# A two-layer decoder on one core: cross queries as three 16-bit products, low values on GpSimd, the expert sum on two engines, a second set of self weights, and a new written order

## What is computed

```
x = x + self_attention0(layernorm(x))        16 heads of 8, causal
x = x + cross_attention0(layernorm(x), ctx)   8 heads of 64, with output bias
x = x + ternary_ffn(layernorm(x))             x rounded to 8 bit, weight rounded to -1, 0, 1
x = x + self_attention1(layernorm(x))        16 heads of 8, scores clipped to +-10, causal
x = x + cross_attention1(layernorm(x), ctx)  16 heads of 64
x = x + experts(layernorm(x))                 8 experts, softmax gate, those under 0.1 dropped
```

## Time and profile before

| | |
|---|---|
| median of 3 runs | 501.73 us (499.9 to 504.64) |
| profiled execution | 504.29 us, span 502.5 us, mean granted TensorE clock 0.983 |
| TensorE busy | 471.4 us, 94% |
| ScalarE busy | 438.6 us, 87% |
| VectorE busy | 404.4 us, 80% |
| GpSimd busy | 383.4 us, 76% |

### The profile page before, as it was taken

The page is one execution under the profiler, slowest core; times in us unless marked ns, Lnnn a source line. Parts: engine busy times, 40 slices in busy tenths (PEclk is TensorE's granted clock), DMA queues, the critical chain, the costliest instruction groups (busy, mean ns, idle before and its releaser), DMA issues.

```text
span 502.5 us, 16468 instructions
## 1 busy us (share of the span) xinstructions
PE 471.4 (94%) x5702; PEld 399.1 (79%) x5702; DVE 404.4 (80%) x954; ACT 438.6 (87%) x1180; POOL 383.4 (76%) x465
## 2 busy tenths in 40 slices
PE   7789998999999999999999999999999899999866
PEld 3678786787888898877888888897788788978764
DVE  4598887986888888888889898888987678867645
ACT  4688889999999989998989999999889898999842
POOL 2487587877668878889979888996877599775752
PEclk8799999998999999999999999999999999999989
DMA  6800222205132422531254215243424224233450
GB/s 195 330 3 3 43 43 44 43 10 115 24 68 45 85 44 42 94 65 39 48 92 87 55 29 79 44 90 46 85 53 84 57 44 86 43 65 71 89 97 16
DMA packets 107841, 33.87 MB, mean 67 GB/s; under 512 B 102768, under 2 KB 106224, under 8 KB 107760
## 3 DMA queue, kind: packets, MB, share of 16 engines
q1 hardware_dynamic: 107328, 32.04, 31.8%
q10 hardware_dynamic: 432, 0.79, 0.5%
HBM read 6.50 MB, written 1.05 MB: 15 GB/s over the span
## 4 chain that ended last, share of the span: by engine, by line
PE 59%; ACT 10%; POOL 9%; issue 9%; DMA 3%; POOLq 3%; DVE 3%; SPq 2%; DVEq 1%; ACTq 0%
PE psum L1291 6%; PE psum L1333 5%; PE psum L1419 5%; PE psum L1342 4%; POOL w_self L774 4%; PE psum L1322 4%; POOL e_parts_cross L781 3%; PE psum L1382 3%; ACT w_cross L865 3%; DMA eT_cross<-e_parts_cross 2%; PE psum L1431 2%; PE psum L1392 2%; PE psum L1373 2%; PE psum L1400 2%; PE psum L1355 2%
## 5 line engine op out<-in xcount | busy, mean ns | idle before, releaser
L774 POOL TENSOR_TENSOR w_self<-w_self 128x1024 f16<-128x1024 f32 x64 | 120.9, 1900 | 19.8 <-ACT w_self L854 14.3
L781 POOL TENSOR_TENSOR e_parts_cross<-w_cross,e_parts_cross 128x1024 f16<-128x1024 f32 x48 | 102.6, 2141 | 13.0 <-ACT e_parts_cross L874 13.0
L865 ACT ACTIVATE w_cross<-psum,row_max_cross 128x128 f32<-128x128 f32 x384 | 105.0, 413 | 3.7 <-DVE row_max_cross L1045 3.4
L1045 DVE TENSOR_REDUCE row_max_cross<-psum 128x8 f32<-128x1024 f32 x48 | 58.3, 1219 | 7.9 <-PE psum L1333 7.5
L1333 PE MATMUL psum<-kT_cross,qT_cross 64*128 64x128 f32 x768 | 54.7, 284 | 0.6 <-ACT qT_cross L830 0.6
L1333 PEld LDWEIGHTS psum<-kT_cross,qT_cross 64*128 64x128 f32 x768 | 46.4, 187 | 8.4 <-issue 5.2
L874 ACT ACTIVATE e_parts_cross<-w_cross 128x1024 f16<-128x1024 f32 x48 | 52.6, 1099 | 0.3
L1373 PE MATMUL psum<-v_high_cross,eT_cross 128*128 128x65 bf16 x384 | 40.6, 196 | 5.5 <-DMA eT_cross<-e_parts_cross 3.7
L1373 PEld LDWEIGHTS psum<-v_high_cross,eT_cross 128*128 128x128 f16 x384 | 35.7, 98 | 10.5 <-issue 8.9
L1083 DVE SCALAR_TENSOR_TENSOR w_self<-psum,s_bound 128x1024 f32<-128x1024 f32 x32 | 37.9, 1219 | 4.3 <-PE psum L1322 3.6
L1072 DVE TENSOR_REDUCE row_max_self<-psum 128x8 f32<-128x1024 f32 x32 | 38.9, 1216 | 2.9 <-PE psum L1322 2.8
(11 more groups left out here) (221 smaller groups left out, 1539.9 us busy)
## 6 DMA issues: line engine op xcount, KB each, us to landing
eT_cross<-e_parts_cross SPq DMA_TRANSPOSE x96, 3.1
out_dram<-x_all SPq DMA_DIRECT2D x16, 64.0 KB, 2.0
x_all<-in_x SPq DMA_DIRECT2D x1, 768.0 KB, 7.8
cT_all<-in_ctx SPq DMA_DIRECT2D x1, 768.0 KB, 9.6
e_k<-in_e_k SPq DMA_DIRECT2D x1, 512.0 KB, 5.5
e_v<-in_e_v SPq DMA_DIRECT2D x1, 512.0 KB, 6.4
e_q<-in_e_q SPq DMA_DIRECT2D x1, 512.0 KB, 8.6
e_o<-in_e_o SPq DMA_DIRECT2D x1, 512.0 KB, 9.6
```

The source lines that it names most:

```text
L774: pool.tensor_tensor(L.w_low[u], L.w[u][:], halves(L.w[u][:]), ALU.subtract)\
L781: pool.tensor_tensor(L.e_parts[u][:, UN:2 * UN], L.e[u][:], L.e_parts[u][:, 0:UN], ALU.subtract)\
L865: last = act.activation(L.e[u][:, P * p:P * (p + 1)], S_[:, P * p:P * (p + 1)], ACT.Exp, bias=L.row_max[:, u, p:p + 1])
L1045: dve.tensor_reduce(L.row_max[:, u, :], group(i, turn)[:].rearrange("p (h k) -> p h k", h=UNIT), AX_X, ALU.max, negate=True).then_inc(L.ma ...
```

## The change

Five edits, with new costs in `all_steps` and a new `ORDER` for every engine:

1. Queries: the weight is scaled by 4096 and split once into a bf16 high part (ScalarE, `b_q.hi` and `e_q.hi`) and an fp16 low part (VectorE, `b_q.lo` and `e_q.lo`); `xnT` of the cross stages is fp16, with an fp16 remainder `xnT_low` made by a new VectorE step `xl`. A query step has twelve 16-bit products instead of four fp32 ones. ScalarE's copy out (`qe`) undoes the scale.
2. Values: ScalarE now writes them as fp32; the bf16 high and fp16 low parts are the upper and lower 16 bits of each 4-byte place, so `pv` reads both with a step of 4 bytes. cross1's `vl` moves to GpSimd; cross0's stays on VectorE.
3. Cross weights: `lo` writes its remainder over the first half of `w`, so the next `ex` waits until the transposing DMA of the remainder has landed (`e_turned`) and no longer for `e_low`; `lo` loses its own wait for that DMA.
4. First self attention: `w` exists twice (four tiles); `mx` waits for the `pv` of two sequences before, and `ex` loses its wait for the previous `pv`.
5. Experts: `ml` multiplies four experts in one instruction of 128x512 and adds the other four with four multiply-add instructions of 128x128; `sm` loses its first addition of 128x512.

`LOADS` puts `e_k`, `e_v` and `ctx` ahead of `more`. Some small tiles move into room that the new tiles leave. The new order keeps the shape of the old one: the same steps run on TensorE, ScalarE's order has the two `hi` steps more, VectorE's has `xl` and the two `lo` steps more and cross1's `vl` less, and GpSimd's has these.

```
+VECTOR_LOW = ("cross0",)
+Q_UNIT = 4096.0
...
-                add(f"{L}.mx.{u}", "DVE", 2430, [f"{L}.s1"], [f"{L}.t.{u}"])
+                add(f"{L}.mx.{u}", "DVE", 2430, [f"{L}.s1"], [ago(f"{L}.pv", 2)])
...
-    add("tern.make", "DVE", 2900, ["tern.sum"], once=True)
+    add("tern.make", "DVE", 5000, ["tern.sum"], once=True)
...
-                     more=["a_o", "b_q", "b_o", "b_bias", "f_w"], e_k=["e_k"], e_v=["e_v"], x=[], ctx=[],
+                     e_k=["e_k"], e_v=["e_v"], ctx=[], more=["a_o", "b_q", "b_o", "b_bias", "f_w"], x=[],
...
-        self.v_high = [self.sb(f"v_high{b}", [P, heads, XD + 1], BF16) for b in range(AHEAD[name])]
-        self.v_low = [self.sb(f"v_low{b}", [P, heads, XD], FP16) for b in range(AHEAD[name])]
+        self.v = [self.sb(f"v{b}", [P, heads, XD + 1]) for b in range(AHEAD[name])]
+        self.v_high = [by_halves(v, BF16)[:, :, :, 1] for v in self.v]
+        self.v_low = [by_halves(v, FP16)[:, :, 0:XD, 0] for v in self.v]
...
+        self.high_plane = [self.sb(f"high_plane{u}", [P, UN], FP16) for u in range(self.units)]
+        self.low_plane = [w[:].bitcast(FP16)[:, 0:UN] for w in self.w]
...
             def low_weights(L, i, u):
                 pool.wait_ge(L.e_high[u], i + 1)
-                if i:
-                    pool.wait_ge(L.e_turned[u], 16 * i)
-                pool.tensor_tensor(L.e_parts[u][:, UN:2 * UN], L.e[u][:], L.e_parts[u][:, 0:UN], ALU.subtract)\
+                pool.tensor_tensor(L.low_plane[u], L.e[u][:], L.high_plane[u][:], ALU.subtract)\
                     .then_inc(L.e_low[u], 1)
+            def low_values(L, i, u):
+                buffer, heads = i % AHEAD[L.name], slice(UNIT * u, UNIT * (u + 1))
+                pool.wait_ge(*emptied(i, f"{L.name}.v.{u}"))
+                pool.tensor_tensor(L.v_low[buffer][:, heads, :], L.v[buffer][:, heads, 0:XD],
+                                   L.v_high[buffer][:, heads, 0:XD], ALU.subtract).then_inc(L.v_split[u], 1)
...
-                pool.tensor_tensor(weighted[:, 0:4, :], weighted[:, 0:4, :], weighted[:, 4:8, :], ALU.add)
-                pool.drain()
...
                 act.wait_ge(L.max_ready[u], i + 1)
                 if i:
-                    act.wait_ge(L.e_low[u], i)
+                    act.wait_ge(L.e_turned[u], 16 * i)
...
+                if name in q_high:
+                    act.activation(q_high[name][:], wt[name][:], ACT.Copy, scale=Q_UNIT).then_inc(hi_ready[name], 1)
+                    return
...
+            def low_queries(name):
+                dve.wait_ge(hi_ready[name], 1)
+                dve.scalar_tensor_tensor(out=q_low[name], in0=wt[name][:], scalar=Q_UNIT, in1=q_high[name][:],
+                                         op0=ALU.mult, op1=ALU.subtract).then_inc(lo_ready[name], 1)
+
+            def low_x(L, i):
+                name = f"{L.name}.xT"
+                dve.wait_ge(L.xnT_ready, i + 1)
+                dve.tensor_tensor(L.xnT_low[:], bank(i, name)[:, 0:P], L.xnT[:], ALU.subtract)\
+                    .then_inc(emptied(i, name)[0], 1)
...
-                dve.tensor_tensor(weighted[:], group(i, "moe.e")[:].rearrange("p (e d) -> p e d", e=EXPERTS),
-                                  g_weight[:, 0:EXPERTS].unsqueeze(2).broadcast_to([P, EXPERTS, P]), ALU.mult)\
-                    .then_inc(taken(i, "moe.e")[0], 1)
+                dve.tensor_tensor(weighted, group(i, "moe.e")[:, 0:4 * P].rearrange("p (e d) -> p e d", e=4),
+                                  g_weight[:, 0:4].unsqueeze(2).broadcast_to([P, 4, P]), ALU.mult)
+                dve.drain()
+                for e in range(4, EXPERTS):
+                    last = dve.scalar_tensor_tensor(out=weighted[:, e - 4, :], in0=group(i, "moe.e")[:, P * e:P * (e + 1)],
+                                                    scalar=g_weight[:, e:e + 1], in1=weighted[:, e - 4, :],
+                                                    op0=ALU.mult, op1=ALU.add)
+                last.then_inc(taken(i, "moe.e")[0], 1)
...
-            def four_pairs(i, name, w, c, xT):
+            def four_pairs(L, i, name, c):
+                w_high, w_low = q_high[f"{L.letter}_q"], q_low[f"{L.letter}_q"]
                 for k in range(4):
-                    col = P * (4 * c + k)
-                    last = pe.matmul(bank(i, name)[:, P * k:P * (k + 1)], w[:, col:col + P], xT,
-                                     start=True, stop=True)
+                    col, out_ = P * (4 * c + k), bank(i, name)[:, P * k:P * (k + 1)]
+                    pe.matmul(out_, w_low[:, col:col + P], L.xnT[:], start=True, stop=False)
+                    pe.matmul(out_, w_high[:, col:col + P], L.xnT_low[:], start=False, stop=False)
+                    last = pe.matmul(out_, w_high[:, col:col + P], L.xnT[:], start=False, stop=True)
                 last.then_inc(x_full, 1)
```

More of the change, by code:

```diff
@@ L178, in all_steps @@
         add(f"{name}.lo", engine, lo, [f"{name}.hi", *(["self0.nm"] if name == "ctx0" else [])], once=True)
+    for name, load, hi, lo in (("b_q", "more", 520, 610), ("e_q", "cross1", 940, 2200)):
+        add(f"{name}.hi", "ACT", hi, [f"in.{load}"], once=True)
+        add(f"{name}.lo", "DVE", lo, [f"{name}.hi"], once=True)
     add("self0.st", "DVE", 440, ["in.x0", "consts", since("in.x1", 1), since("in.x", EARLY)], ["self0.rs"])
@@ L1413, in cross_project @@
                     room(i, y)
+                if i == 0 and c == 0:
+                    load = "more" if L is cross0 else "cross1"
+                    pe.wait_ge(loaded[load], load_count(load))
                 with_x = L is cross1 and i == NSEQ - 1
```

244 lines of the change are left out of this document (133 added, 111 removed).

## The result

| | changed kernel | kernel before |
|---|---|---|
| median | 501.46 us of 20 runs | 504.05 us of 20 runs |
| ratio | 0.9929 [0.9903, 0.9956] | |
| profiled execution | 500.77 us, span 498.5 us, mean granted clock 0.989 | 504.29 us, span 502.5 us, 0.983 |

Six slow runs of the changed kernel are left out of the ratio: three at 849 to 2384 us, and three at 505 to 507 us with the lowest mean granted clocks (0.976 to 0.979). The change takes 0.7% off, about 3.6 us (2.2 to 4.9 by the interval); the forecast was 10.5, taken off 501.7 us, a median of three runs, where 20 runs give 504.05. The parts were mostly priced well where the trace had a row for them. What failed is the step from a part to the end of the kernel.

The account below looks back on a forecast made before the run. TensorE's own work was taken to bound the kernel between 150 and 350 us, its waits elsewhere. Queries -6.3, start -2.9, order -3.7 and cross weights +2.4 made -10.5, on the 501.7 median 491 us; range 481 to 505.

Parts of the forecast that it names:

- Queries: TensorE's 48 query steps as twelve 16-bit products, 0.71 us a step against 0.89: -6.3 us, ends -9.6 and +13.9.
- Start: First 20 us, earlier e_k load: TensorE's wait behind ScalarE gone, -2.9 us, ends 0 and -6.9.
- Splits of the weights: One-off query weight splits on ScalarE and VectorE: costed at nothing; uncovered +1.6 and +2.0 us.
- xl: VectorE's low activations ahead of the cross queries, about 0.27 us each: costed at nothing; uncovered +8.6 us.
- Order and second set: New order and second self weights, 20 to 150 us: half of TensorE's idle gone, -3.7 us, ends -7.4 and +6.2.
- Cross weights at the end: Last exponentials wait for the remainder's transposing DMA to land: +2.4 us, ends 0 and +4.7.
- they wait for a DMA: Sign of a right forecast, at the kernel's end: the last exponentials wait for a DMA.
- Strided values: TensorE's value products reading 2 bytes of every 4: costed at nothing; a second pass over the columns would be +34 us.
- VectorE and GpSimd: Side work: VectorE -2.0 on 404, GpSimd from 383 to 396 us; no change to the time.
- 81 ns: The skill's spacing for 128-column weight load and product: a query step 0.97 us, term +3.9, time an estimated 501.
- Swallowed: Rival: the cut doesn't reach the end, engines in fixed order block each other; 500 us, chance 0.19 for 496.7 to 506.7.
- GpSimd late, ScalarE held: Rival: in the middle, remainders queue behind low values, land late and ScalarE stands at ex; around 510 us, chance 0.10.

Follow-up runs that it names:

- before_q5: Kernel before with each fp32 query product replaced by five 16-bit products of the upper halves; 10.2 us slower by level, 9.4 by ratio.
- before_q3: Kernel before, old order, with each fp32 query product replaced by three 16-bit products of the upper halves; 0.7 us less by ratio, 1.3 by level.
- experiment 1: Two runs: 16-bit query products alone in the kernel before (0.7 us less than before), and the query part undone in the changed kernel (1.6 more than the change).
- after_fp32q: Changed kernel with its query part undone: fp32 query products, no query weight splits, no xl; 1.6 us more than the change, level 500.9 us.
- before_loads: Kernel before with only the loads reordered, e_k, e_v and ctx ahead of more; 2.9 us less by ratio, 2.7 by level.
- after_bq_early: Changed kernel with VectorE's b_q.lo moved earlier, between two row maxima; 497.41 us median, ratio 0.986 to the kernel before.
- after_act: Changed kernel with ScalarE's 16-bit copy of the exponentials halved from the second sequence on; 1.4 us less at an equal clock, 1.1 by ratio.
- after_all3: Changed kernel with one query product of three, ScalarE's exponentials copy halved, and first row maxima over 48 keys; 12.3 us less at an equal clock, 490.9 us median.
- before_loads_q3: Kernel before with the loads reordered and three 16-bit query products of the upper halves; 3.2 us less by ratio.

## Why the forecast failed

**Queries: the failing step.** The prediction read "between 150 and 350 us it is busy 198.1 of 200: time there is TensorE's own work, and every product saved is time saved", counted 22 steps fully and 26 half, and came to -6.3 us. "Every product saved is time saved" is what failed. The step was even shorter than forecast, 10.2 us in all, and the end moved by 0.7 us [-0.8 to 2.2] in the old order, 1.3 by level, while TensorE's idle time grew by 5.0. A busy share near 1 went with more work costing its length (`before_q5`), and not with less work gaining. Put as two lines, with TensorE's work at its full price on its own line: at its old work TensorE's line is 514.3 - 9.9 = 504.4 us, and the kernel before stands on it; with the three products it would be 494.2, and `before_q3` stands 8.6 above, at 502.8, held by other chains of waits. So only 1.3 us of room lay under the old time. Which chain holds it isn't shown; the wait that grew most is the one ahead of the value products (experiment 1). In the changed kernel that wait is long too, most of it with no releaser in the profile:

```profile
L1433 PE MATMUL psum<-v_cross,eT_cross 128*128 128x65 bf16 x384 | 42.2, 196 | 8.5 <-issue 5.6 <-DMA eT_cross<-w_cross 1.3 <-DMA eT_cross<-high_plane_cross 0.8
```

In the new order the same sum goes: 504.1 before; 500.9 with all but the query part (`after_fp32q`); some 495.8 with the shorter products alone (by difference, no run); plus 2.1 for `xl` and 2.5 for the blocked split, 500.4. Counted with slope 1, as `before_q5` shows it in the old order (in the new one it is an assumption), TensorE's line under the change is 524.7 - 31.9 = 492.8, or 490.3 without the 2.5 us for which the split keeps TensorE idle; with the 10.3 us of the fp32 steps that is 500.6, near the 500.9 of `after_fp32q`. By this estimate TensorE's line fell by 11.6 us, about what the sum of the prediction said, and the change stands 7.6 above it. The forecast was made of TensorE's line alone; the other chains' had to be asked for too.

**Start:** -2.9 forecast, -2.9 measured (`before_loads`): the mechanism was right, and the agreement to the tenth is luck, with an interval of 1.5 to 4.3. **Splits of the weights:** 0 forecast, with 2.0 as the uncovered end on VectorE; the one of `b_q` took 3.93 us and cost 1.7 to 3.5. A row had hinted at it: the earlier trace rows has a 128x128 operation at 2.25 us, read only as a late step and not as a blocked one. In the kernel before it ended 0.08 us after GpSimd's split of `e_v`, the first line here; in the changed kernel the same operation, the second line, met no GpSimd operation that reads and took 0.23:

```profile
27.32 2.37 POOL L643 TENSOR_TENSOR e_v_lo<-e_v,e_v_hi 128x1024 fp32r<-128x1024 f32 x1
...
29.22 0.23 DVE L1252 TENSOR_SCALAR ternary<-w_cross 128x128 bf16<-128x128 f32 x1
```

For operations like the split of `b_q`, the Trainium skill ("SBUF — State Buffer", section "SBUF: two separate sides") says that a VectorE operation with two SBUF inputs and a GpSimd operation that reads SBUF exclude each other for a whole instruction; the trace agrees, with 3.93 us beside GpSimd's 3.48 us subtraction and 0.68 where GpSimd ran only a 0.55 us operation on 128x1 (`after_bq_early`). That short one began first and didn't hold the split, so there the rule isn't seen.

**`xl`:** 0 forecast, 8.6 if uncovered, 2.1 to 2.3 measured. **Order and second set:** -3.7 forecast; the second set alone is worth 2.6 to 3.4 in the new order. But `after_fp32q`, which has all of the change except the query part, stands at 500.9 where `before_loads` has 501.4 (by ratio it is 0.9 slower): beyond the loads, order, second set and side work together gave nothing near 3.7. What the order is worth by itself wasn't tried. **Cross weights at the end:** +2.4 forecast and not found. The sum had the second remainder end at 473.66 + 3.0 = 476.7; it ended at 467.73 + 2.14 = 469.9, since the new order has the first one done some 10 us earlier. Its transposing DMA, issued at 469.89, lands 3.2 us later (the median of these), at about 473.1, and the last exponentials begin at 473.29 against 476.08, right behind ScalarE's copy. So the sign "they wait for a DMA" was wrong, by some tenths of a us. In the kernel before, too, they stood right behind the copy (last line), and not behind a remainder:

```profile
467.73 2.14 POOL L810 TENSOR_TENSOR w_cross<-w_cross,high_plane_cross 128x1024 f16<-128x1024 f32 x1
469.89 1.94 SPq L733 DMA_TRANSPOSE eT_cross<-w_cross  x1
472.31 1.06 ACT L907 ACTIVATE high_plane_cross<-w_cross 128x1024 f16<-128x1024 f32 x1
473.29 2.17 ACT L898 ACTIVATE w_cross<-psum,row_max_cross 128x128 f32<-128x128 f32 x8
...
475.12 1.06 ACT L874 ACTIVATE e_parts_cross<-w_cross 128x1024 f16<-128x1024 f32 x1
```

**Strided values:** some 1.6 us of TensorE's time in place of 0, not priced by a run. VectorE and GpSimd came to 407.9 and 397.0 us (402 and 396 forecast). Query products at 55 ns speak against the 81 ns that the prediction takes from the Trainium skill.

**Rivals.** *Swallowed* is what happened: the cut doesn't reach the end, since other engines' chains lay just below. That its 500 us is near the 501.46 measured is luck, for its terms were others: it kept the queries' 6.3 and put the start at nothing. Its evidence was ScalarE's 188.3 of 200, in the same row as the argument against it. That ScalarE is what holds the end isn't shown: 15.9 us less of its work gave 1.4 (`after_act`). *GpSimd late, ScalarE held* found no support: ScalarE's list of waits in the changed kernel has no transposing DMA (in `after_all3`, with three engines' work cut, it has one, 1.0 us in all).

## What to carry to other kernels

Before work is taken off the fullest engine, ask how far below the next chain lies; one run with work added and one with work taken out price both sides, and a balanced kernel can show a knee. In this kernel two stalls in the first 40 us came off the end at about their length (2.9 us for 2.93, and 1.7 to 3.5 for 2.86), while an engine's busy time taken out gave much less than its length. Before a one-off VectorE step with two SBUF inputs is placed, look at what GpSimd does at that moment.

## What the runs showed of the hardware

The spread of the runs goes with TensorE's mean granted clock, which differs from run to run of the same program (0.980 to 0.997 for `before_loads_q3`): 0.41 us for each 0.001. The start of the two profiled executions differs so too: in the first 20 us the granted clock was 0.80 of full speed before, a mean of stretches at 2.4 and at 1.2 GHz, and 1.00 (2.4 GHz) after. The change isn't the reason, since `before_q3`, which loads as the kernel before does, had 1.00 there too.

Blocking went both ways: GpSimd's low-value operation at 34.84 us, which met the rest of the `b_q` split, took 1.49 us in place of 1.06, and its 0.55 us power operation 1.53 us at 53.49, beside the split of `e_q`.
